# A two-layer decoder on one core: block mask by DMA after the ReLU, sorting steps moved behind copies, start and last unit reordered

## The reference

```
x += attn0(LN(x))        # one head of 256, causal, weights qk and ov
x += xattn0(LN(x), ctx)  # 16 heads of 16, mask given (all false here)
x += ffn0(LN(x))         # 16 blocks of 64 hidden; top 4 blocks per token
x += attn1(LN(x))        # 16 heads, qkv, o and a residual inside
x += xattn1(LN(x), ctx)  # 16 heads, windows of 64 + previous, rotary, token match
x += moe1(LN(x))         # 8 experts of 128, top 2 by sigmoid, plus a shared MLP

ffn0: mask = top_k(softmax(x @ w_router + b_router), 4) as 0/1 per block
      h = relu(x @ w1.T + b1);  y = (h * mask of its block) @ w2.T + b2
```

## Time and profile before

| | us |
|---|---|
| median of 3 runs | 791.42 |
| profiled execution | 791.41 |
| its span | 789.6 |
| mean granted TensorE clock | 0.996 |

### The profile page before, as it was taken

The page is one execution under the profiler, slowest core; times in us unless marked ns, Lnnn a source line. Parts: engine busy times, 40 slices in busy tenths (PEclk is TensorE's granted clock), DMA queues, the critical chain, the costliest instruction groups (busy, mean ns, idle before and its releaser), DMA issues.

```text
span 789.6 us, 17005 instructions
## 1 busy us (share of the span) xinstructions
PE 755.5 (96%) x6045; PEld 615.4 (78%) x6045; DVE 521.3 (66%) x1418; ACT 425.0 (54%) x1254; POOL 330.8 (42%) x457
## 2 busy tenths in 40 slices
PE   7999999999899999999999999999999999999997
PEld 6887777776688888877777777777777767888886
DVE  4675788887622343137767767788899987567655
ACT  2445677777532222337777766677665667323320
POOL 3233333443323222314222216666678745715550
PEclk9999999999999999999999999999999999999999
DMA  8902234322042226000000003000000001235539
GB/s 312 390 5 75 75 100 120 79 75 75 15 134 74 74 78 145 14 1 2 1 2 2 2 2 121 15 15 15 15 15 28 28 29 48 87 96 162 162 109 319
DMA packets 57569, 61.46 MB, mean 78 GB/s; under 512 B 21296, under 2 KB 48176, under 8 KB 56464
## 3 DMA queue, kind: packets, MB, share of 16 engines
q1 hardware_dynamic: 54080, 51.03, 21.2%
q0 software_dynamic: 3408, 9.34, 3.5%
HBM read 31.10 MB, written 29.27 MB: 76 GB/s over the span
## 4 chain that ended last, share of the span: by engine, by line
PE 63%; DVE 17%; issue 7%; POOL 7%; ACT 4%; DMA 2%; SPq 1%; POOLq 0%; DVEq 0%; ACTq 0%
PE pj L366 8%; PE pj L373 8%; PE pj L460 7%; PE ov L536 7%; PE sc L523 7%; PE sc L449 6%; DVE mx L1005 5%; POOL routed_y L1770 5%; PE ov L471 4%; PE pj L360 4%; DVE pT L1012 2%; PE sc L444 2%; ACT pr L1499 2%; PE sc L666 2%; DVE sc L998 2%
## 5 line engine op out<-in xcount | busy, mean ns | idle before, releaser
L1499 ACT ACTIVATE pr<-sc,mx 128x128 f32<-128x128 f32 x768 | 216.6, 395 | 82.3 <-DVE mx L1005 80.1
L1005 DVE TENSOR_REDUCE mx<-sc 128x4 f32<-128x512 f32 x192 | 125.6, 683 | 38.5 <-PE sc L449 36.4
L460 PE MATMUL pj<-idn,pr 128*128 128x128 f32 x768 | 121.3, 283 | 5.4 <-DVE pT L1012 1.3
L460 PEld LDWEIGHTS pj<-idn,pr 128*128 128x128 f32 x768 | 83.9, 141 | 44.5 <-issue 24.9
L1012 DVE COPY pT<-pj 128x512 f32<-128x512 f32 x128 | 87.1, 686 | 31.9 <-PE pj L460 31.6
L1687 POOL TENSOR_SCALAR ve<-mv 128x2 f32<-128x2 f32 x40 | 14.1, 352 | 185.4 <-DVE mv L936 184.9
L1517 ACT ACTIVATE hT<-sc,vecs 128x256 f32<-128x256 f32 x64 | 30.3, 473 | 90.6 <-PE sc L523 90.6
L523 PE MATMUL sc<-xnT,W 128*128 128x256 f32 x256 | 64.1, 380 | 0.0
L536 PE MATMUL ov<-W,hT 128*128 128x256 f32 x256 | 60.5, 381 | 0.0
L449 PE MATMUL sc<-kM,qT 32*128 32x256 f32 x768 | 55.0, 400 | 4.4 <-ACT pr L1499 4.0
L1482 ACT ACTIVATE pT<-pj 128x512 f32<-128x512 f32 (+1 forms) x72 | 42.0, 585 | 27.6 <-PE pj L460 27.0
(11 more groups left out here) (227 smaller groups left out, 1537.1 us busy)
## 6 DMA issues: line engine op xcount, KB each, us to landing
sorted_x<-more_xT SPq DMA_DIRECT2D x15, 1152.0 KB, 6.9
kM<-sorted_x SPq DMA_DIRECT2D x39, 129.0 KB, 2.1
cT<-in_ctxT SPq DMA_DIRECT2D x16, 256.0 KB, 3.4
W<-in_w SPq DMA_DIRECT2D x2, 1024.0 KB, 13.6
cT<-in_ctx SPq DMA_DIRECT2D x8, 256.0 KB, 3.0
W<-in_w_gu SPq DMA_DIRECT2D x1, 2048.0 KB, 8.0
hT<-routed_y SPq DMA_DIRECT2D x8, 256.0 KB, 5.7
out_x<-X SPq DMA_DIRECT2D x8, 256.0 KB, 3.9
```

The lines of the kernel that those rows point to most:

```text
L460: last = tr(bank[b][:, i * S:(i + 1) * S], pr[n % 4][:, i, :], idn[:])
L1005: v.tensor_reduce(mx[n % 4][:], four(b), AX.X, ALU.max, negate=True).then_inc(mx_done, 1)
L1499: last = a(pr[n % 4][:, i, :], bank[b][:, i * S:(i + 1) * S], ACT.Exp, bias=mx[n % 4][:, i:i + 1])
```

## The change

- Start: `memset` of `va` in four pieces at unit 3, not two at unit 1. Pair 2 of x is loaded alone ahead of `Wov`. x_norm(2) stands ahead of softmax0(0); small constants are made at unit 1.
- ffn0: `expb`, its input and the matmul go. `nm` now has 1 for each kept block. ScalarE copies its f32 transpose at the end of the unit before. SyncE stores its 16 rows in DRAM (`kept_at`), waits for that, and loads them with each row repeated over 64 partitions, in eight DMAs, into four tiles (`pr` or `pT`, idle in this stage). VectorE multiplies `hT` by them in four instructions of 128x512.
- Sorting: `settle` moves behind the copy of the unit's first turned probabilities, `choose` from `part2` to `part3` behind `head_stats`. `picked`, `counted`, `ones`, `strict` are bf16 for `rank` and `totals`; GpSimd casts two constants at unit 34.
- After the last unit: `gate(5)` and `turn_out` ahead of the first shared product on TensorE, `gates(5)` ahead of the first SiLU on ScalarE, the first `shared_gated` later on VectorE, one scatter of four behind the last inverse on GpSimd.
- End: one semaphore for the two loads of a pair of `routed_y`.

```diff
 # up2 / down2 (TensorE)
                 if c == 0:
-                    pe.wait_ge(*emptied("nm", U))
-                mm(bank[b][:, 0:T], expb[:, c * P:(c + 1) * P], nmT[U % 2], start=True, stop=False)
+                    pe.wait_ge(*emptied("xT", U))
...
-                    pe.wait_ge(*emptied("h", U, d))
+                    pe.wait_ge(kept_hidden, 4 * (U % PAIRS) + d // 2 + 1)
 # VectorE
-                v.tensor_scalar(nm[:, :, 0:NB], kept[:, :, 0:NB], -1.5, None, ALU.is_gt).then_inc(nm_done, 1)
+                v.tensor_scalar(nm[:, :, 0:NB], kept[:, :, 0:NB], -1.5, None, ALU.is_lt).then_inc(nm_done, 1)
+            def keep_hidden(U, q):
+                p = U % PAIRS
+                if q == 0:
+                    dve.wait_ge(s_keep[U % 2], 128 * (p // 2 + 1))
+                dve.wait_ge(*emptied("h", U, 2 * q + 1))
+                some = hT[U % 2][:, 2 * q:2 * q + 2, :]
+                v.tensor_tensor(some, some, keep[U % 2][q], ALU.mult).then_inc(kept_hidden, 1)
 # half (VectorE)
                 elif f == 0 and j == 0:
+                    if U == 0:
+                        x_norm(2)
                     softmax0(U)
 # part0 -> part1: settle
-                if late(U, 36) is not None:
-                    settle(late(U, 36))
+            def part1(U):
                 if late(U, 36) is not None:
                     settle(late(U, 36))
 # part2 -> part3 (behind head_stats): choose
-                if late(U, 35) is not None:
-                    choose(late(U, 35))
...
                     head_stats(U, 0)
+                if late(U, 35) is not None:
+                    choose(late(U, 35))
             def alone0(U):
+                if stage(U) == 2 and U % PAIRS >= 2:
+                    keep_hidden(U, 0)
             def alone1(U):
+                if stage(U) == 2:
+                    for q in range(int(U % PAIRS >= 2), 4):
+                        keep_hidden(U, q)
 # ScalarE, part3, ahead of the copy of xT
+                if stage(U + 1) == 2:
+                    if (U + 1) % PAIRS >= 2:
+                        act.wait_ge(s_kept, 16 * ((U + 1) % PAIRS - 1))
+                    copy_out(nmT[(U + 1) % 2], "nm", U + 1)
 # GpSimd
-                if U == 1:
+                if U == 3:
                     for r in two:
-                        g.memset(va[r][:], 0.0).then_inc(s_ones, 1)
-                    pool.wait_ge(s_ones, 2)
+                        for j in two:
+                            g.memset(va[r][:, j], 0.0).then_inc(s_ones, 1)
+                    pool.wait_ge(s_ones, 4)
...
+                if U == 4 * PAIRS + 2:
+                    pool.wait_ge(s_w[5], 6 * 16)
+                    g.tensor_copy(strictb[:], strict[:]).then_inc(s_counts, 1)
+                    g.tensor_copy(onesb[:], ones[:]).then_inc(s_counts, 1)
...
-            scatter(4)
+            scatter(4, which=((0, 0), (0, 1), (1, 0)))
             inverse(mv5[1], ve5, rstd5[1], mv5_done, ve5_done, rstd5_done, 7)
+            scatter(4, which=((1, 1),))
 # SyncE, once per pair, behind the ctx load and the blank rows
+            def spread(U):
+                p = U % PAIRS
+                sp.wait_ge(*emptied("nm", U))
+                sp.dma_start(kept_at[p], nmT[U % 2][0:NB, :]).then_inc(s_kept, 16)
+                sp.wait_ge(s_kept, 16 * (p + 1))
+                if p == 0:
+                    sp.wait_ge(*full("pT", U - 1, 7))
+                elif p == 1:
+                    sp.wait_ge(*full("O", U - 2, 1))
+                else:
+                    sp.wait_ge(kept_hidden, 4 * (p - 1))
+                for h in two:
+                    rows_of = kept_at[p].rearrange("(c h) t -> h c t", h=2)[h]
+                    for i, some in enumerate(keep[U % 2]):
+                        sp.dma_start(some[h * BLOCK:(h + 1) * BLOCK], rows_of[2 * i:2 * i + 2].unsqueeze(0)
+                                     .to_broadcast([BLOCK, 2, T])).then_inc(s_keep[U % 2], 16)
 # TensorE, after the last unit
             probs_times_values(Z, 1)
+            gate(5)
+            turn_out(Z, 1)
             shared_up(0, 0)
-            turn_out(Z, 1)
-            gate(5)
+            turn_heads(Z)
             rank(4)
-            turn_heads(Z)
+            output4(Z)
             shared_up(0, 1)
-            output4(Z)
 # VectorE, after the last unit
-            shared_gated(0, 0)
             norm_heads(Z, 1)
...
             norm5(6)
-            shared_gated(0, 1)
+            shared_gated(0, 0)
             residual("o", Z)
             stats5(7)
+            shared_gated(0, 1)
             shared_gated(1, 0)
```

More of the change, by code:

```diff
@@ L68, with program @@
 NROW = sum(n for _, n in ROWS.values())
-def program(nc, x, ctxT, ctx, tokq, tokk, mask, ident, causal, expand, vec, rows, lnb, before, blank,
+def program(nc, x, ctxT, ctx, tokq, tokk, mask, ident, causal, vec, rows, lnb, before, blank,
             w_qk, w_ov, w_q0, w_k0, w_v0, w_r0, w_1, w_2, w_qkv, w_o1, w_x, w_g, w_gu,
-            w_down, ws_gate, ws_up, ws_down, sorted_x, routed_y, out):
+            w_down, ws_gate, ws_up, ws_down, kept_at, sorted_x, routed_y, out):
     stack = ExitStack()
@@ L206, in program @@
         nm = sb("nm", [P, 2, P])
-        nmT = [mask4[:].rearrange("p b s -> p (b s)").bitcast(BF16)[:, r * T:(r + 1) * T] for r in two]
+        nmT = [mask4[:].rearrange("p b s -> p (b s)").bitcast(F32)[:, r * T:(r + 1) * T] for r in two]
+        keep = [[t[:].rearrange("p a s -> p (a s)").rearrange("p (c t) -> p c t", t=T) for t in ring] for ring in (pr, pT)]
         sg = [t[:].rearrange("p j s -> p (j s)") for t in sh]
@@ L218, in program @@
         share, comb = sb("share", [P, B, TOPE]), sb("comb", [P, B, TOPE])
-        picked = [sb(f"picked{r}", [P, 2, E]) for r in two]
-        picked_sum = sb("picked_sum", [P, E])
-        counted = sb("counted", [P, PAIRS + 1, E])
+        picked = [sb(f"picked{r}", [P, 2, E], BF16) for r in two]
+        picked_sum = sb("picked_sum", [P, E], BF16)
+        counted = sb("counted", [P, PAIRS + 1, E], BF16)
         strict = sb("strict", [P, P])
@@ L269, in program @@
         s_yt = [sem(f"s_yt{r}") for r in range(4)]
-        s_routed = [sem(f"s_routed{b}") for b in range(B)]
+        s_routed = [sem(f"s_routed{p}") for p in range(PAIRS)]
+        s_kept, kept_hidden = sems("s_kept kept_hidden")
+        s_keep = [sem(f"s_keep{r}") for r in two]
         sg_done = sem("sg_done")
@@ L654, in totals @@
                 pe.wait_ge(counted_done, 2 * PAIRS + 1)
-                mm(bank[b][:, 0:E], ones[:], counted[:, PAIRS, :], start=True, stop=True).then_inc(filled[b], 1)
+                mm(bank[b][:, 0:E], onesb[:], counted[:, PAIRS, :], start=True, stop=True).then_inc(filled[b], 1)
             def shared_up(p, e, sides=two):
@@ L1312, in part1 @@
             def part1(U):
+                if late(U, 36) is not None:
+                    settle(late(U, 36))
                 if stage(U + 1) == 4:
@@ L1324, in part1 @@
                     inverse_sums0(U - 1)
-                if stage(U) == 0:
+                if stage(U) == 0 and U > 0:
                     x_norm(U + 2)
@@ L1516, in hidden2 @@
                 act.wait_ge(filled[b], n)
+                if c == 0 and U % PAIRS >= 2:
+                    act.wait_ge(*full("y2", U - 2))
                 a(hT[U % 2][:, c, :], bank[b][:, 0:T], ACT.Relu, bias=V("b1", c)).then_inc(drained[b], 1)
@@ L1645, in _ @@
             copy_out(oT[1][:], "O", Z, 1)
+            gates(5)
             shared_silu(0, 0)
-            gates(5)
             copy_out(hdT[Z % 2], "hT", Z)
@@ L1753, in count, with scatter @@
                 g.tensor_tensor(counted[:, p + 1, :], counted[:, p, :], picked_sum[:], ALU.add).then_inc(counted_done, 1)
-            def scatter(p, U=None):
+            def scatter(p, U=None, which=((0, 0), (0, 1), (1, 0), (1, 1))):
                 if p == 0:
@@ L1759, in scatter @@
                 pool.wait_ge(slot_done, 3 * p + 3)
[L1760 to L1765, removed]
+                for j, k in which:
+                    if U == 5 * PAIRS - 1:
+                        pool.wait_ge(*full("pT", U, 4 + TOPE * j + k))
+                    g.indirect_dma_start(sorted_x, bass.IndirectOffsetOnAxis(slot_of[:, p, j, k:k + 1], 0),
+                                         xw[p % 4][:, j, :], None).then_inc(s_scatter[p % 4], 16)
             def tile_scatter(t):
@@ L1882, in _ @@
                 sp.dma_start(dst[:], src).then_inc(s_w[1], 16)
[L1883 removed]
+            for dst, src in ((Wr0[:], w_r0), (W1[:], w_1), (W2[:], w_2)):
                 sp.dma_start(dst, src).then_inc(s_w[2], 16)
@@ L1984 @@
             "cosk": np.cos(ak).astype(one)[:, turned], "sink": (np.sin(ak) * sign).astype(one)[:, turned]}
-    expand = np.zeros((P, FF * P), one)
-    for b in range(NB):
-        expand[b, b * BLOCK:(b + 1) * BLOCK] = NEG
     causal = np.where(np.tril(np.ones((S, S), bool)), 0.0, NEG).astype(one)
```

50 lines of the change are left out of this document (22 added, 28 removed).

## The result

The changed kernel takes 787.03 us (median of 20 runs, 785.72 to 792.58), the kernel before 791.02 us (20 runs, 789.93 to 792.60): ratio 0.9954, 95% interval 0.9943 to 0.9966. That is 4.0 us less; forecast were 7.4 us less (784.0). The profiled execution of the changed kernel took 789.23 us (span 787.4), 2.2 us above its own median; its granted clock averages 0.988, that of most other runs 0.991 (before: 0.996).

A forecast was written before the change was run, and what follows sets the result against it. TensorE was taken to bound the block FFN, VectorE to be busiest in the sorting attention; -6.9 - 2.2 + 6.0 - 3.1 - 1.7 + 0.5 = -7.4 gave 784.0 us, own range 780 to 788, whole range 776.5 to 788.5.

The forecast's parts named there:

- stage 2: Block FFN: 64 matmuls removed from a full TensorE, -6.9 us (bounds 0 and -7.1), the replacement staying hidden.
- t = 8: Sign: all eight mask loads landed by then, counted in us from unit 21's first down product; 7.2 was assumed.
- Start: Pair 2's earlier statistics bring unit 1's first scores from 17.70 to 15.5: -2.2 us (bounds -1 and -2.6).
- Cost 0: Block FFN: mask store, loads and VectorE products stay hidden, ending 4 us before TensorE's transpose, so they add no time.
- rival B: Mask loads land after t = 11.4, each unit becomes a loop; at 14.0 it costs 15.6 us: 799.6. Chance 0.10.
- rival C: Block FFN saving given back at the unit's edge, where down products wait for their masked halves: 791. Chance 0.06.
- The lock: GpSimd's 1.27 us addition to X can hold VectorE's mask products: up to 1.3 of 4 us slack goes, sum unchanged.
- Sorting: Last attention: moved choose +2.3, held choose +1.0, settle +2.4, unit 38 -0.3, casts +0.6; sum +6.0 us (bounds -3, +8).
- Rival A: Sorting gains where the forecast charges it: -1 us instead of +6, total 777. Chance 0.22.
- Last unit: Unit 39: last pair's transpose 2.3 us earlier, shorter counting -0.8; sum -3.1 us (bounds -1 and -4).
- End: Two loads instead of one before the first diagonal product: +0.5 us.
- Clock: Two low-clock stretches, each behind a TensorE gap; gaps shrink and one stretch goes: -1.7 us (bounds 0 and -3.4).

The follow-up runs named there:

- m2: The kernel before with only the kept-blocks mask moved to DMA and VectorE, plus the end's pair-wise semaphores: 789.26 us, ratio 0.9950 (second chip).
- c2: b1 with GpSimd's additions to X in unit 16 held until its four products are done, and the two casts at unit 22: 784.65 us, 0.9881 (third chip).
- b1: s3 with the three late products of a block-FFN unit ahead of the instruction that folds or centres a weight: 788.58 us, ratio 0.9929 (second chip).
- c3: c2 with the last unit in the order of the kernel before: 784.76 us, ratio 0.9886 (third chip).
- m3: The kernel before with only the order of the last unit changed, counting still f32: 793.68 us, ratio 0.9990 (second chip).
- s1: The changed kernel with choose alone back at its old place ahead of the copy: 783.67 us, ratio 0.990.
- s4: The changed kernel with counting products in f32, issued three times over for the first four pairs, as filler in TensorE's gap: 789.73 us, ratio 0.9974.
- s3: The changed kernel with choose and settle both in their old places: 781.51 us, ratio 0.9878.
- c1: s3 run again on the third chip: 788.63 us, ratio 0.9940 to the kernel before.
- s2: The changed kernel with settle alone back at its old place ahead of the copy: 786.73 us, ratio 0.9944.
- m1: The kernel before with only the start changed: 789.68 us, ratio 0.9959 (second chip).
- c4: c2 with settle split in units 36 to 39, first product ahead of the copy, eight small instructions behind the norm: 786.22 us, ratio 0.9903 (third chip).

## Why the prediction came out as it did

The median of 787.0 lies in the range that the prediction gave (776.5 to 788.5) and moved the way it said, by 4.0 of the 7.4 us; the one traced execution, 789.2, lies outside. That the median came out inside is in part luck, for the largest term was not what happened. The prediction's own sign said "I am wrong if stage 2 gives under 5 us": stage 2, its largest term, gave 2.4 in the trace; the eight loads had not landed by t = 8, down products did wait for VectorE in three units, and the last transpose came 1.1 us nearer and not 2.3. The signs of the start and of the sorting held: first scores at 15.0, sorting units 25.0 and 24.5 us long.

- **Start: right.** 2.7 us earlier scores against 2.2, and the low stretch gone, of which half of 3.4 was counted. That the order of the start took it away is not shown (m2).
- **Stage 2: the mechanism right, the cover wrong in three places.** "Cost 0" was true of five units (17, 19, 21, 22 and 23): a product takes 0.61 to 0.69 undisturbed, the period of unit 22 is 15.37, the transpose never waits. Even the three late products of unit 22, which take 3.57 us beside GpSimd's additions, keep no one waiting. The loads land at t = 9.0 (unit 21) and 10.1 (units 22, 23) and not at 7.2: each is issued in 0.64 us and not 0.46, and a load lands 3.2 to 3.3 us (median) after its issue and not 2.1. The unit's first product waits 3.07 for them (row of 292.44; before, the norm stood at 293.37); still under 11.4, so rival B did not occur. What failed is "at most 0.3 us" for unit 16, where the loads end just when VectorE and GpSimd both want to start, and that I never looked at what stands ahead of the late products in units 18 and 20, though I had put the three products "following the residual": there they followed `unfolded(3)` and `centered(3)`. That is rival C in part. c2, b1 and c3 price it: unit 16 2.0, unit 18 0.5, unit 20 0.85, and 0.9 from a low clock (c2 against c3). 6.67 - 2.0 - 0.5 - 0.85 - 0.9 = 2.4, measured 2.4.
- **The lock.** The prediction took the rule from the Trainium skill, "SBUF — State Buffer", section "SBUF: two separate sides", and estimated with it that up to 1.3 of the 4 us go. The trace agrees with the rule (four products 4.21 us beside two GpSimd additions, 2.49 without), but my conclusion that the sum stays was wrong in unit 16, where there is no 4 us of slack.
- **Sorting: right in sum.** Choose 3.3 forecast, 3.5 in the traces; settle 2.4 and 1.7; the casts 0.6 and 0.40 (with the casts moved, the step between units 34 and 35 is 0.03). 0.9 us of low clock in unit 36 was not foreseen. The statement that unit 37's choose costs 0.15 was wrong (1.3); GpSimd's addition held choose's copy for 0.56 us each time (0.73 for 0.17), near the upper bound. Rival A is refuted.
- **Last unit: 3.6 for 3.1, but by other terms.** The last transpose came 1.1 us earlier and not 2.3: VectorE meets the third gated product, which waits 1.20 for ScalarE, ahead of the last norm. Behind it 2.5 us are won: rank 7 and the totals take 0.11 us and not 0.72, rank 6 0.13 and not 0.83 (the latter at the low clock), and the low clock at 673 is gone. On the other two chips no gain of the new order was measured (m3, c2 against c3).
- **End.** +1.5 in the one trace; in the four traces of s1 to s4, with the same loads, the same step is -0.5, 0.0, -0.7 and -0.3. No steady cost.
- **Clock.** Both low stretches of before went and new ones came. Counting it as a fixed price failed: what a low clock costs depends on whether TensorE would have waited behind it.

c2, the old sorting order and three edits, is most likely the best version: 0.988 of the kernel before on a chip where s3's kernel (c1) has 0.994; the changed kernel has 0.995 where it was timed, and s3 0.988 on the first chip. c2 and the changed kernel were not run on one chip; that c2 is faster rests on s3, which beats the changed kernel's ratio on the first chip, and on c1 to c2.

## What to carry to other kernels

When work moves to an engine that is "idle most of the time", read its queue at the edge of every unit that differs from the ordinary one (first, last, those with extra duties): one waiting instruction in front makes all that slack useless. A low clock beside a gap can be a passenger: it cost nothing in two units where TensorE had to wait behind it anyway, and 0.85 and 0.9 us in two places where it had not. Before it is blamed, look at a run that has the gap and the full clock. An instruction is cheap behind a copy only if whoever waits for the next thing in that queue has slack; here, taking two such moves back was worth about 6 us (ratio 0.9954 to 0.9878), more than the whole change gained.

## What was not expected of the hardware

The same gap of 1.84 us ahead of the last transposes of unit 15 (near 200 us) stands in all fourteen kernels. It was followed by a low granted clock in the changed kernel, s1 to s3, b1, c1, c2 and c4 (mean of 196 to 204 us 0.79 to 0.90) and in m2 (0.79 over 200 to 208), and by none in the kernel before, s4, m1, m3 and c3, though c2 and c3, for one, are the same kernel up to there. Nor were the gaps of s1 (1.73 to 1.75 us, three times) and s2 (1.87 to 2.14, three times) followed by it, and in unit 36 of s4 the clock fell with no gap of half a microsecond before it. What decides is not known from these traces.

In the last unit, on two of three chips, ScalarE and VectorE stood idle for 2 to 5 us with no engine to wait for (releaser "remote" or "issue"), more so in the new order (9 to 15 us in sum on ScalarE in m3, b1, c1, c2 and c4) than in the old (2.0 to 2.7 in m1, m2 and c3), and not at all in the traces of the first chip. In b1, c1, c2 and m3 single SiLUs began up to 5 to 7 us after their input was done, in the changed kernel and s1 to s4 0.9 to 1.1. This may be why the new order of the last unit gained in the changed kernel and not there. An exchange of ScalarE's tables stands near each, but whether that, the code's own loading or the scatters is the cause was not tried and stays open.
